# Two transformer blocks on one core: the last attention's keys and values computed during the MLP, in pairs of tiles

## The reference

```
# block 0: cross attention and MLP
xn, yn = layernorm(x), layernorm(ctx)
q, k, v = xn @ Wq, yn @ Wkv            # 16 heads of 16
x = x + softmax(q k / 4) v @ Wproj + bproj
x = x + gelu(layernorm(x) @ W1 + b1) @ W2 + b2      # hidden width 1024
# block 1: cross attention on the RAW context
q = (x * rsqrt(mean(x * x) + eps) * norm_w) @ wq
k, v = ctx @ wkv                        # needs neither x nor a layernorm
q, k = rotate(q), rotate(k)             # rotary position
q, k = q / |q|, k / |k|                 # per head
out = x + softmax(4 q k) v @ wout
```

## Time and profile before

| | |
|---|---|
| median of the runs | 389.51 us |
| span of the profiled execution | 386.9 us |
| its instructions | 11499 |
| PE, weight loads, VectorE, ScalarE, GpSimd busy | 92%, 82%, 76%, 62%, 51% |
| TensorE clock granted | at full speed throughout |

### The profile page before, as it was taken

One profiled execution on the slowest core, in us unless ns is written; L12 is line 12 of the kernel. 1 busy time (PEld: TensorE's weight loads), 2 busy tenths in 40 slices (PEclk: granted clock), 3 DMA queues, 4 the chain that ended last, 5 costly groups with the idle time before them and its releaser, 6 DMA issues.

```text
span 386.9 us, 11499 instructions
## 1 busy us (share of the span) xinstructions
PE 356.5 (92%) x4475; PEld 318.7 (82%) x4475; DVE 294.4 (76%) x654; ACT 239.3 (62%) x464; POOL 197.1 (51%) x177
## 2 busy tenths in 40 slices
PE   8998999999999989898999999978889989989974
PEld 5977888888888867798999998978778878878854
DVE  4799987989899773267755559467899999999752
ACT  2356677666677655815644476163877777777862
POOL 2474544554665611003331233248899998999810
PEclk9999999999999999999999999999999999999999
DMA  6853001110000000000000000000001001010001
GB/s 157 246 158 121 27 25 43 32 28 25 2 3 4 22 2 2 2 2 0 0 0 0 0 0 3 10 22 0 22 12 36 26 26 42 29 37 14 29 30 41
DMA packets 14432, 12.39 MB, mean 32 GB/s; under 512 B 2996, under 2 KB 13752, under 8 KB 14392
## 3 DMA queue, kind: packets, MB, share of 16 engines
q1 hardware_dynamic: 14384, 11.83, 10.4%
q10 hardware_dynamic: 8, 0.00, 0.0%
HBM read 9.73 MB, written 2.10 MB: 31 GB/s over the span
## 4 chain that ended last, share of the span: by engine, by line
PE 58%; issue 22%; DVE 10%; ACT 5%; POOL 4%; POOLq 0%; DVEq 0%; ACTq 0%
PE bank_qk L697 9%; PE banks_s L745 6%; PE bank_y L834 4%; PE bank_y L828 3%; PE banks_s L1032 3%; PE bank_t L800 3%; PE bank_qk L722 3%; PE bank_o L736 3%; PE bank_t L697 3%; PE bank_qk L726 3%; DVE row_max L1203 2%; POOL x_all L375 2%; PE bank_y L1052 2%; PE bank_o L1021 2%; PE bank_y L929 1%
## 5 line engine op out<-in xcount | busy, mean ns | idle before, releaser
L413 POOL TENSOR_TENSOR norm_inv<-norm_sq_min,minus_half 128x32 f32<-128x32 f32 x16 | 87.5, 5468 | 1.8 <-DVE norm_sq_min L1374 1.8
L576 ACT ACTIVATE W_s<-banks_s,b_cols 128x256 f32<-128x256 f32 x60 | 25.0, 469 | 41.3 <-PE banks_s L915 41.3
L342 POOL TENSOR_TENSOR masked<-qkT_r,halves_t 128x512 fp32r<-128x512 f32 x32 | 32.9, 1050 | 24.1 <-DVE qkT_r L1193 24.1
L477 ACT ACTIVATE PT<-banks_s 128x1024 f32<-128x1024 f32 x32 | 31.0, 1022 | 20.3 <-PE banks_s L782 18.3
L1203 DVE TENSOR_REDUCE row_max<-banks_s 128x8 f32<-128x1024 f32 x32 | 37.6, 1218 | 7.7 <-PE banks_s L745 7.7
L368 POOL TENSOR_TENSOR b_var_eps<-b_mean_var,eps_t 128x2 f32<-128x2 f32 x8 | 1.6, 197 | 69.1 <-DVE b_mean_var L1137 69.1
L915 PE MATMUL banks_s<-lnT_hi,W_hi 128*128 128x256 f32 x120 | 34.2, 285 | 0.0
L915 PE MATMUL banks_s<-lnT_hi,W_lo 128*128 128x256 f32 x120 | 33.9, 283 | 0.0
L915 PE MATMUL banks_s<-lnT_lo,W_hi 128*128 128x256 f32 x120 | 33.9, 283 | 0.0
L642 ACT ACTIVATE PT<-banks_s 128x1024 f32<-128x1024 f32 x32 | 31.1, 1024 | 4.1 <-PE banks_s L1032 4.1
L745 PE MATMUL banks_s<-masked,qkT_r 32*128 32x256 f32 x768 | 31.5, 294 | 1.6 <-DVE row_max L1203 1.3
(11 more groups left out here) (171 smaller groups left out, 1095.6 us busy)
## 6 DMA issues: line engine op xcount, KB each, us to landing
ctx_in<-in_ctx SPq DMA_DIRECT2D x32, 96.0 KB, 2.0
x_all<-in_x SPq DMA_DIRECT2D x16, 128.0 KB, 2.1
W_s<-in_L_xattn_W SPq DMA_DIRECT2D x2, 1024.0 KB, 6.4
out<-Wq_s SPq DMA_DIRECT2D x16, 128.0 KB, 1.8
Wq_s<-in_L_xattn_Wq SPq DMA_DIRECT2D x1, 256.0 KB, 3.0
Wkv_s<-in_L_xattn_Wkv SPq DMA_DIRECT2D x1, 256.0 KB, 3.2
Wproj_s<-in_L_xattn_Wproj SPq DMA_DIRECT2D x1, 256.0 KB, 4.2
wout_s<-in_L_xattn_wout SPq DMA_DIRECT2D x1, 256.0 KB, 3.0
```

The costliest lines, as they stand in the source:

```text
L342: nc.gpsimd.tensor_tensor(masked[:, r, 1, :, half, :], qkT_r[:, r, 1, :, :].bitcast(fp32), ones, ALU.mult)\
L413: nc.gpsimd.tensor_tensor(norm_inv[:, j, :], norm_sq_min[:, j, :], minus_half[:, :], ALU.pow)\
L477: nc.scalar.activation(PT[:, 2 * h:2 * h + 2, :], banks_s[:, 2 * h:2 * h + 2, :], ACT.Exp, scale=HD ** -0.5)\
L576: last = nc.scalar.activation(hT[:, m, :], (bank or bank_s[u])[:, 256 * k:256 * k + 256], ACT.Gelu, bias=b1_cols[:, m:m + 1])
```

## The change

The keys and values of the last attention need only the raw context, so they are computed for all tiles in the MLP stage, two tiles at a time.

- The context is passed transposed as an extra input, `ctx_T`; GpSimd splits it (`context_hi`, `context_lo`). The context transposes go. The results of all tiles stay in SBUF (`keysT`, `vals_c`); the first attention's buffers are released and reused.
- Keys of two tiles fill one bank, values of two tiles another, with 256 columns a matmul. Rotation, norms and transposes run on two tiles at once. The queries too are made by pairs.
- The scores are made with 8 fp32 matmuls a tile and no split.
- The queries' RMS factor cancels in the head norm: only its epsilon is kept, through `clamp_c` and the maximum in `queries_sums`.
- The hidden layer of the MLP uses two banks, `bank_s[0]` and `bank_s[1]`, in turn. The splits of `wkv` move from VectorE to GpSimd in the first attention.
- All loops are written out, and the order of every engine from the MLP on is new.

```diff
@@ TensorE
+            def keys_c(p, bank):
+
+                pe.wait_ge(c_ctx_lo, p + 1)
+                for j in range(2):
+                    last = split_mm(bank[:, in_pair(j, C1)], ctxT_r[:, :, :, in_pair(j, TOK)], wkv_r[:, :, :, 0:C1])
+                last.then_inc(c_kv, 1)
...
+            def inputs_c(p, bank):
+
+                pe.wait_ge(b_x, 2 * p + 2)
+                turned_pair(bank, x_all[:, in_pair(p, 2), :].rearrange("p b c -> p (b c)")).then_inc(c_xT, 1)
...
+            def scores_c(t):
+
+                p, j = t // 2, t % 2
+                pe.wait_ge(c_masked, 2 * p + 2)
+                pe.wait_ge(c_keys, p + 1)
+                for k in range(KT):
+                    for g in range(NG):
+                        last = mm(bank_s[g][:, in_pair(k, 2 * TOK)], keysT[quad(g), k, in_pair(t, TOK)],
+                                  masked_q[quad(g), p % 2, k, :, in_pair(j, TOK)], start=True, stop=True)
+                        if k == KT - 1:
+                            last.then_inc(C["scores"], 1)
...
+            pe.wait_ge(b_gelu, 13)
+            up_b(3, 2, bank_s[0])
...
+            pe.wait_ge(c_keys, 2)
+            keys_T(2, bank_qk)
@@ GpSimd
+            def context_hi(p):
+
+                r = p % 2
+                pool.wait_ge(ctx_loaded[r], 2 * LOADED * (p // 2 + 1))
+                wait(pool, c_kv, p)
+                wait(pool, c_v_mm, p)
+                nc.gpsimd.tensor_copy(ctxT_r[:, 0], ctx_in[:, 2 * r:2 * r + 2, :]).then_inc(c_ctx_hi, 1)
...
+            def keys_norms(p):
+
+                pool.wait_ge(c_kmin, p + 1)
+                wait(pool, c_kunit, p)
+                nc.gpsimd.tensor_tensor(norm_k_inv[:, :], norm_k_min[:, :], minus_half[:, :], ALU.pow).then_inc(c_kinv, 1)
@@ ScalarE
+            def gelu_b(p, u, bank):
+
+                act.wait_ge(b_w1, 4 * p + u + 1)
+                wait(act, b_hT_lo, 4 * p + u - 3)
+                for k in range(2):
+                    m = 2 * u + k
+                    last = nc.scalar.activation(hT[:, m, :], bank[:, in_pair(k, 256)], ACT.Gelu, bias=b1_cols[:, m:m + 1])
+                last.then_inc(b_gelu, 1)
...
+            def queries_out(p, bank):
+
+                act.wait_ge(c_qT, p + 1)
+                wait(act, C["scores"], NG * (2 * p - 2))
+                for half in range(2):
+                    nc.scalar.activation(masked_q[:, p % 2, :, half, :], joined(bank[:, :]), ACT.Copy, scale=halves_t[:, half:half + 1])\
+                        .then_inc(c_masked, 1)
@@ VectorE
+            def keys_units(p):
+
+                dve.wait_ge(c_kinv, p + 1)
+                v.tensor_tensor(heads(rot_k, 2 * H), heads(rot_k, 2 * H), each(norm_k_inv[:, :], 2 * H, HD), ALU.mult).then_inc(c_kunit, 1)
...
-            pipeline(dve, step_c, 3, STEPS_C, peeled=10)
```

More of the change, by code:

```diff
@@ L55 @@
 QUARTERS = 4
-def known(n):
-    return isinstance(n, int)
 def ok(tile):
-    return not known(tile) or 0 <= tile < NB
+    return 0 <= tile < NB
 def wait(eng, sem, count):
-    if not known(count) or count > 0:
+    if count > 0:
         eng.wait_ge(sem, count)
 def upto(tile):
[L75 to L90, removed]
+    return min(tile, NB)
 def build(nc, x, ctx, ln1_w, ln1_b, ln2_w, ln2_b, ln3_w, ln3_b, Wq, Wkv, Wproj, bproj, W1, b1, W2, b2,
-          norm_w, wq, wkv, wout, rope, halves, picks, out):
+          norm_w, wq, wkv, wout, ctx_T, rope, halves, picks, out):
     es = ExitStack()
@@ L424, in _ @@
+            queries_norms(7)
         @block.scalar
@@ new lines, in exps_c, with out_T_c @@
+            def exps_c(t):
+                act.wait_ge(C["scores"], NG * t + NG)
+                wait(act, C["av"], t)
+                for h in range(2):
+                    nc.scalar.activation(PT[:, 2 * h:2 * h + 2, :], banks_s[:, 2 * h:2 * h + 2, :], ACT.Exp, scale=HD ** 0.5)\
+                        .then_inc(C["exped"], 1)
+            def out_T_c(t, bank):
+                act.wait_ge(C["av"], t + 1)
+                wait(act, C["o_back"], t)
+                nc.scalar.activation(oT[:, :], bank[:, :], ACT.Copy).then_inc(C["oT_ready"], 1)
@@ L829, in project_a, with turn_b @@
                     last.then_inc(A["proj_mm"], 1)
[L831 to L838 removed]
+            def turn_b(p, bank):
                 pe.wait_ge(b_norm, 2 * p + 2)
@@ L934, in _, with down_b @@
+            def down_b(p, j, u, bank):
+                pe.wait_ge(b_hT_lo, 4 * p + u + 1)
+                for m in (2 * u, 2 * u + 1):
+                    for n, (h, w) in enumerate(((hT_hi, W2_hi), (hT_hi, W2_lo), (hT_lo, W2_hi))):
+                        last = mm(bank[:, 0:C1], h[:, m, 128 * j:128 * j + 128], w[:, m, :],
+                                  start=m == n == 0, stop=m == HM - 1 and n == 2)
+                last.then_inc(b_down[j], 1)
             queries_keys_a(NB - 1)
@@ new lines, in normed_c, with project_c @@
+            def normed_c(t, bank):
+                pe.wait_ge(C["on_ready"], t + 1)
+                for k in range(KT):
+                    last = nc.tensor.transpose(bank[:, 128 * k:128 * k + 128], on[:, 128 * k:128 * k + 128], ident[:, :])
+                last.then_inc(C["on_transposed"], 1)
+            def project_c(t, bank):
+                pe.wait_ge(c_onT_lo, t + 1)
+                split_mm(bank[:, 0:C1], onT_r[:, :, :, :], wout_r[:, :, :, :]).then_inc(C["proj_mm"], 1)
+            pe.wait_ge(w2_lo_done, 4)
```

1578 lines of the change are left out of this document (1107 added, 471 removed).

## The result

The changed kernel takes **367.87 us** (median of 4 runs, 367.57 to 368.43) against 389.49 us (4 runs, 388.66 to 389.62) of the kernel before beside it: ratio 0.948, 95% interval 0.943 to 0.952. I had said 374.3, with 365 to 387 as the range. The direction, the places and the order of the sizes were right; the sum was 6.4 us too high, and it was made of larger errors in both directions.

A forecast was written before the change was run, and what follows sets the result against it. PE was taken as the MLP's wall, four engines as nearly full in the last attention, with 30 us of waits. 283.1 + 50.9 + 4.6 + 21.0 + 12.1 = 371.7 us span, plus 2.6: 374.3 us, range 365 to 387.

The forecast's parts named there:

- (a): PE's work: 32 context transposes go, -3.4 us; key, value and query matmuls keep their number and width.
- (b): Last attention's scores as 8 fp32 matmuls: 0.91 us a tile, near end 0.87, far end 3.47 if serial.
- R3: Rival: fp32 scores run one after another, 2.56 us more per tile, 415 us, slower; chance 0.07.
- (c): MLP with all tiles' keys and values: 15.2 us a pair on PE, no stall, margins 0.8 to 1.3 us.
- R1: Rival: waits fill back into the MLP, 1.5 us in 6 pairs, 9 us, 383 us; chance 0.12.
- (d): First scores of the last attention at 283.1 us, including 4 us of waits at both ends of the MLP.
- (e): Last attention's tiles: ten periods 50.9 us plus 4.6 for lost time, five late periods 21.0, tail 12.1.
- the slip of 4.6 us: First ten tile periods: today's steady-step loss, 0.66 of 7.31 us or 9%, added as 4.6 us.
- R2: Rival: no slip, the 9% loss in the tiles doesn't come, 370 us; chance 0.13.
- The ring: From the tenth tile on, exponentials, values, next scores and hand-overs decide: 4.2 us a period, five of them 21.0.
- (f): The rest, such as weight splits moved to GpSimd in first attention: nothing, or 0.5 us in each of 8 steps.
- R4: Rival: first ten tiles stay at 7.3 us behind GpSimd's powers, 392 us, slower by 0.6%; chance 0.05.

The follow-up runs named there:

- e1: Kernel before with its loops written out and nothing else changed; ratio to before 0.997 (0.992 to 1.002).
- e5: Kernel before with the last attention's scores as 8 fp32 matmuls instead of 24 fp32r ones, no low parts made; ratio to before 0.997 (0.992 to 1.002).
- e4: Changed kernel with four idle transposes ahead of each of the eight key products; span without the start 360.4 us against 356.5.
- e8: Changed kernel with an idle 512-column ScalarE pass behind the exponentials of the last attention's first ten tiles; first to last scores 75.1 us against 74.7.
- e6: Changed kernel with a second buffer for exponentials and a new order from tile 9 on; span without the start 354.8 us against 356.5.
- e3: Changed kernel with four idle transposes ahead of the projection of tiles 8 to 12; span without the start 358.3 us against 356.5.
- e12: Changed kernel with second buffers for exponentials and output tiles, a new last part, and late weight splits moved off VectorE's casts and centring products; ratio to before 0.943.
- e9: Changed kernel with GpSimd's weight splits in first-attention steps 12 to 15 waiting for VectorE's rounding of the row maxima; ratio to before 0.953 (0.946 to 0.960).
- e7: Changed kernel with an unused 16-column power on GpSimd ahead of each keys' power; span without the start 372.7 us against 356.5.

## Why the prediction was right, and where it was off

**What bounds it.** Right in the main. PE was full in the MLP and 30 us of waits stood behind it. After, PE's own work from the same row on is 190.4 - 3.4 + 2.6 = 189.6 us and the last product ends 200.6 us behind it: 11 us of waits are left, where I had forecast 18. Filled waits are the gain. e1 and e5, which leave the work in its place, bring nothing; no run moves the keys and values alone. Not right was to read the tiles as bound by four engines nearly full: e5 takes a sixth of VectorE's work away and nothing gets shorter. PE's list itself held them. The wait of 0.66 us stands between PE's weighted values and its next transposes, with one eviction on ScalarE between the two; that row of before, from all engines in order of time:

```profile
325.65 0.38 ACT L623 ACTIVATE vals<-bank_t 128x256 f32<-128x256 f32 x1 [0.69 <-PE bank_y L834]
```

By the code this eviction waits for the weighted values (`wait(act, C["av"], t - 1)`), since `vals` has two buffers, and the transposes wait for it, since they write the same bank. So a tile was PE's own 6.65 us and this round trip; e5 agrees, its 0.16 us of PE work lengthen the tile by 0.16.

**(a) Context transposes.** -3.4 us. e4 puts as many into the MLP and loses 3.8, which supports their price on a full PE; what they cost in the tiles of before was not measured.

**(b) Scores.** They overlap, so R3 is out. But the size was off: 1.07 us (278.43 to the next row's 279.50), not 0.91 nor the 0.87 of four sequential rounds. 16 x 0.16 = 2.6 us. The range's far end, 3.47, was right to keep: no row of before had this form. By the Trainium skill, TensorEngine Tiling (Array Packing), section Tiling Modes, tiles run side by side; the row agrees in kind (1.07 against 3.47 in sequence), and is 0.2 us over what four perfect rounds would take.

**(c) MLP.** 15.2 us a pair predicted; GpSimd's powers of two neighbouring pairs show it to the hundredth:

```profile
205.84 5.43 POOL L439 TENSOR_TENSOR norm_k_inv<-norm_k_min,minus_half 128x32 f32<-128x32 f32 x1 [0.67 <-DVE norm_k_min L1921]
221.04 5.43 POOL L439 TENSOR_TENSOR norm_k_inv<-norm_k_min,minus_half 128x32 f32<-128x32 f32 x1 [0.67 <-DVE norm_k_min L1921]
```

The power ran at 5.43, its own 5.47, and the bias addition, which I feared at 1.10, came down to 0.74. R1 did not happen, by 1.6 us.

**(d) First scores.** PE in order of time, after:

```profile
162.53 0.60 PE L1070 MATMUL bank_o<-ident,b_xn 128*128 128x128 f32 x4
...
165.85 0.83 PE L930 MATMUL bank_o<-wkv_r,ctxT_r 128*128 128x256 f32 x5 [0.59 <-POOL ctxT_r L432]
...
278.43 1.15 PE L1244 MATMUL banks_s<-masked_q,keysT 32*128 32x256 f32 x16
279.50 0.66 PE L1212 MATMUL bank_qk<-ident,rot_q 128*128 128x128 f32 x4
```

278.43 - 162.53 = 115.9 us. The work alone is 894 matmuls and 76 transposes, which the trace has in just these numbers, 115.3 us. **The step that failed is the 4 us of waits "at both ends of the MLP"**: there is one wait of 0.6 us. I had carried the changeover of before into an order that fills it with key and value products.

**(e) Tiles.** Ten periods 52.7 us, 55.5 predicted. The work was 50.9 + 10 x 0.16 = 52.5, so the slip of 4.6 us is 0.2 (PE's listed waits are one of 0.32 and one of 0.24): R2's case, to which I had given 0.13. I took the 9% from a steady step with three engines at 92%, and reckoned ScalarE 90% full in the new ones; it is at 79%, and e8 shows that even 88% costs almost nothing. Five late periods: 22.0 us, 21.0 predicted. The ring was the right one for the three short periods (e6 breaks it), its terms 4.41 us in place of 4.2: the way from scores' start to exponentials is 1.29 in place of 1.04. The row of before already had 375.95 - 374.84 = 1.11; my 0.13 counts from the end of the row's 0.98 and was added to 0.91. The other two periods, 4.48, are PE's own work (e3). Tail 12.5, 12.1 predicted.

**(f) The rest at nothing.** For the `wkv` splits I had kept "if the cover went, 0.5 us in each of 8 steps" as the far end. The cover was there, GpSimd had room; what I had not seen is that its work can block VectorE. It cost 1.9 us, and e12 has them back.

In the sum: predicted span 371.7, measured 365.7. The start -3.1, first attention +1.9, to the first scores -3.4, ten periods -2.8, five periods +1.0, tail +0.4: -6.0. From the profiled span to the median are 2.2 us, not 2.6; around the span of one execution lie 1.8 to 1.9 in both (388.66 against 386.9, 367.57 against 365.7), the rest is that the other executions differ. Half of the error was not the kernel's but TensorE's rate at the start of the two profiled executions. Without the start the forecast would be 2.9 us too high: 6.2 too high in the middle and 3.3 too low elsewhere, and that these partly cancel is luck. R4 (ten tiles at 7.3) is out at 5.3.

What stays open: the round trip that held before's tiles is read from rows and code; no run cut it by itself, by a third buffer for `vals` or another order. e1 and e5 exclude the loops and VectorE's load.

## What to carry to other kernels

Move work to the stage where its engines idle, and count PE's instructions there: a stage that is full on PE is predictable to 1%, and a slip seen beside full engines does not carry over once they have room. Where two buffers or one decide a ring, write the ring's terms out before adding anything. And read short instructions of VectorE that are suddenly long against GpSimd's rows: order between two engines can matter with no semaphore between them.

## What the runs showed of the hardware

- An fp32 product of 32 rows and 256 columns, eight a tile on four row groups: 16 instructions in 1.07 us.
- A VectorE cast from SBUF to SBUF stands still until GpSimd's subtraction ends, also one that starts just behind it: 0.17 us became 1.40 to 1.80, and 0.17 again when the subtraction was moved (e9). VectorE's operations with two inputs in SBUF suffer too: two centring products 2.25 in place of 0.87 us. GpSimd's powers took 5.43 to 5.80 us in the changed kernel and did not hold up VectorE's sums of two SBUF tiles (0.69 us).
- TensorE's rate at the start differs between executions: the same 26 transposes take 3.06, 4.41 or 5.81 us, and the real work starts 3 to 4 us later. Comparing stages from the first row that uses loaded data makes differences of 0.2 us readable from single profiles.
- After a wait of PE of 2.30 us (e5) and 2.14 us (e7) the granted clock fell to half for some 3 us and cost about 1.4 us; before has the same wait of 2.30 us and no fall.
